# Gate and up products of batches 0 and 1 made joint, the short transform for batch 0, and new instruction sequences on every engine of a decoder layer

## What is computed

```
h = layernorm(x)
q, k, v = h Wq' + bq, h Wk' + bk, h Wv' + bv      # 16 heads of 16
qp, kp = elu(q) + 1, elu(k) + 1
attn = qp (kp' v) / (qp . sum(kp) + 1e-6)          # per head
x = x + attn Wo' + bo

score = (ctx Wq2' + bq2)(ctx Wk2' + bk2)' / 8 * layernorm(x)
x = x + softmax(where(mask, -inf, score))

h = fwht(layernorm(x) * SU_ug) / 64                # transform over 256
up, gate = h W_up' * s_up, h W_gate' * s_gate      # 256 -> 1024 each
h = fwht(silu(gate) * up * SU_dp) / 64             # transform over 1024
x = x + h W_down' * s_down                         # 1024 -> 256
```

## Time and profile before

| | |
|---|---|
| median of 3 runs | 125.3 us (125.2 to 125.59) |
| the profiled execution | 125.14 us |
| its span | 123.3 us |
| TensorE busy | 119.2 us, 97% |
| DVE, ACT, POOL busy | 82.7, 71.6, 68.5 us |

### The profile page before, as it was taken

The page is one execution under the profiler, slowest core; times in us unless marked ns, Lnnn a source line. Parts: engine busy times, 40 slices in busy tenths (PEclk is TensorE's granted clock), DMA queues, the critical chain, the costliest instruction groups (busy, mean ns, idle before and its releaser), DMA issues.

```text
span 123.3 us, 2272 instructions
## 1 busy us (share of the span) xinstructions
PE 119.2 (97%) x804; PEld 107.0 (87%) x804; DVE 82.7 (67%) x207; ACT 71.6 (58%) x158; POOL 68.5 (56%) x89
## 2 busy tenths in 40 slices
PE   5999999999999999999999999999999999999990
PEld 2259999999999999999989999988888888889890
DVE  1399989899889899899998959674522332220521
ACT  1785696679748689888491479983135444280000
POOL 2228959979979966959802605762005574066000
...
DMA packets 3823, 7.64 MB, mean 62 GB/s; under 512 B 544, under 2 KB 1952, under 8 KB 3684
## 3 DMA queue, kind: packets, MB, share of 16 engines
...
## 4 chain that ended last, share of the span: by engine, by line
PE 97%; POOL 0%; DVE 0%; issue 0%; POOLq 0%
PE bank L1283 19%; PE bank L1295 18%; PE bank L1300 11%; PE bank L1177 10%; PE bank L1304 5%; PE bank L1201 5%; PE bank L1239 5%; PE bank L1155 4%; PE bank L1115 4%; PE bank L1211 3%; PE bank L1221 3%; PE bank L1309 2%; PE bank L1146 2%; PE bank L1247 2%; PE bank L1128 1%; PE bank L1259 1%
## 5 line engine op out<-in xcount | busy, mean ns | idle before, releaser
L1283 PE MATMUL bank<-xh_home,wug 128*128 128x256 f32 x192 | 24.7, 285 | 0.0
L1283 PEld LDWEIGHTS bank<-xh_home,wug 128*128 128x128 f32 x192 | 23.6, 191 | 0.1
L1295 PE MATMUL bank<-xh_home,wug 128*128 128x512 f32 x96 | 22.0, 390 | 0.0
L1295 PEld LDWEIGHTS bank<-xh_home,wug 128*128 128x128 f32 x96 | 18.0, 188 | 3.7
L969 DVE SCALAR_TENSOR_TENSOR back<-bank,sc_up,back 128x512 f32<-128x512 f32 x8 | 6.0, 751 | 15.0 <-PE bank L1295 15.0
L351 POOL TENSOR_TENSOR hs<-back,hs 128x256 fp32r<-128x256 f32 x8 | 5.9, 740 | 17.0 <-ACT hs L614 16.9
L345 POOL TENSOR_TENSOR hs<-front,hs 128x256 fp32r<-128x256 f32 x16 | 11.5, 740 | 6.6 <-ACT hs L599 6.6
L1177 PE MATMUL bank<-watt,xT 128*128 128x256 f32 x96 | 14.0, 288 | 0.0
L1177 PEld LDWEIGHTS bank<-watt,xT 128*128 128x128 f32 x96 | 12.3, 189 | 0.9 <-ACT xT L492 0.7
L606 ACT ACTIVATE back<-bank,vecs 128x512 f32<-128x512 f32 x8 | 5.5, 688 | 12.1 <-PE bank L1295 12.1
L1300 PE MATMUL bank<-wdh,hs 128*128 128x512 f32 x48 | 12.5, 396 | 0.0
...
## 6 DMA issues: line engine op xcount, KB each, us to landing
...
```

The source lines that it names most:

```text
L1283: ins = mm(dst[:, n * SEQ:(n + 1) * SEQ], wug[:, wa, k, at_col + j * P:at_col + (j + 1) * P], xh[b][:, xb, k, :], start=(i == 0), stop=(i ...
L1295: ins = mm(dst[:, :].rearrange("p (b s) -> p b s", s=SEQ), wug[:, wa, k, at_col + j * P:at_col + (j + 1) * P], xh_home[:, PAIR, cols], sta ...
```

## The change

- Gate and up of batches 0 and 1 are joint as well: `gate_up(n)` for n = 0 to 15 replaces both old forms. Its first call waits for XH of both batches. `silu`, `hidden`, `h_hi` and `h_lo` work on the pair (the ring `sg` of 2 x 256 columns in `back`), and the odd batch of a pair has a tile `hs_odd` of its own.
- Batch 0's transform takes the short form; `mix` moves from the tile `ek` to `wo_raw`; `had_x` goes.
- `HEAD` and `SIDE` become one list `ORDER`; `down` is split in H (high products of a tile), L (low products), E (the last of the eight blocks) and F (the last tile). The sequences of DVE, ACT and POOL are new. J is `warm`: 8 before `mx`, then 1 and 5.

```
-HEAD = (("mx", 0), ("u", 0), ("T1", 0), ("u", 1), ("K", 0), ("V", 0), ("Q", 0), ("T1", 1), ("SC", 0),
...
+ORDER = (
+    ("J", 8), ("mx", 0), ("J", 1), ("J", 5), ("u", 0), ("T1", 0), ("u", 1), ("SC", 0), ("K", 0), ("V", 0), ("T1", 1),
+    ("Q", 0), ("ST", 0), ("K", 1), ("NUM", 0), ("V", 1), ("T1", 2), ("AT", 0), ("Q", 1), ("OUT", 0), ("ST", 1),
+    ("V", 2), ("NUM", 1), ("SC", 2), ("K", 2), ("AT", 1), ("Q", 2), ("T1", 3), ("OUT", 1), ("V", 3), ("SC", 1),
+    ("T3", 0), ("ST", 2), ("K", 3), ("NUM", 2), ("SC", 3), ("Q", 3), ("AT", 2), ("ST", 3), ("NUM", 3), ("T3", 1),
+    ("WD", 0), ("XH", 0), ("AT", 3), ("OUT", 2), ("WD", 1), ("XH", 1), ("WD", 2), ("OUT", 3), ("GG", 0), ("GG", 1),
+    ("GG", 2), ("GG", 3), ("GG", 4), ("WD", 3), ("GG", 5), ("GG", 6), ("GG", 7), ("T3", 2), ("H", 0), ("T3", 3),
+    ("L", 0), ("H", 1), ("XH", 2), ("H", 2), ("L", 1), ("E", 0), ("H", 3), ("XH", 3), ("L", 2), ("E", 1), ("E", 2),
+    ("L", 3), ("E", 3), ("GG", 8), ("GG", 9), ("GG", 10), ("GG", 11), ("GG", 12), ("GG", 13), ("GG", 14), ("GG", 15),
+    ("H", 4), ("H", 5), ("L", 4), ("H", 6), ("L", 5), ("E", 4), ("E", 5), ("L", 6), ("E", 6), ("F", 7),
+)
...
             def silu(n):
-                wait_full(act, "GU", n)
+                wait_full(act, "GG", n, 0)
                 if n == 0:
-                    act.wait_ge(s["ug_lo"], 2)
+                    act.wait_ge(s["ug_lo"], 4)
                 if n >= RING:
-                    act.wait_ge(s["h_lo"], n - RING + 1)
+                    act.wait_ge(s["h_lo"], 2 * (n - RING) + 2)
...
+            def gate_up(n):
+                q, j = n // JB, n % JB
                 if j == 0:
+                    for b in range(2 * q, 2 * q + 2):
+                        wait_read(pe, "XH", b)
+                if n == 0:
+                    pe.wait_ge(s["ug_lo"], 2)
+                if n == JB // 2:
+                    pe.wait_ge(s["ug_lo"], 4)
+                for t, at_col in enumerate((INTER, 0)):
+                    dst = take("GG", n, t)
                     for i, (k, wa, xb) in enumerate(PASSES):
                         cols = slice(xb * FB * SEQ + k * SEQ, xb * FB * SEQ + (k + 1) * SEQ)
                         ins = mm(dst[:, :].rearrange("p (b s) -> p b s", s=SEQ), wug[:, wa, k, at_col + j * P:at_col + (j + 1) * P],
+                                 xh_home[:, 2 * q:2 * q + 2, cols], start=(i == 0), stop=(i == len(PASSES) - 1))
+                    done(ins, "GG", n, t)
```

More of the change, by code:

```diff
@@ L32 @@
 BANKS = 8
-WARM, WARM_MORE = 8, 2
 MASKED = 3.0e35
@@ L650, in _ @@
+            exp_q(2)
             xT_hi(3)
-            at_hi(1)
-            negate_mean(3, 0)
-            score_evac(2)
-            exp_q(2)
             normalise(3, 0, xn3)
+            ug_hi(2)
+            table(ACT.Exp, 1)
+            mix_in(0)
+            ug_hi(3)
+            prob(1)
             x3_hi(0)
+            exp_k(3)
             score_evac(3)
-            exp_k(3)
-            prob(1)
+            exp_q(3)
+            at_hi(2)
+            pre_hi(0)
+            negate_mean(3, 1)
@@ L660, in _ @@
+            normalise(3, 1, xn3)
+            pre_hi(1)
+            mix_in(1)
+            x3_hi(1)
+            wd_hi(0)
             xh_hi(0)
-            ug_hi(2)
-            exp_q(3)
-            pre_hi(0)
+            at_hi(3)
+            xh_hi(1)
+            wd_hi(1)
             silu(0)
-            pre_hi(1)
-            negate_mean(3, 1)
+            wd_hi(2)
+            prob(2)
             silu(1)
-            ug_hi(3)
             silu(2)
-            normalise(3, 1, xn3)
-            table(ACT.Silu, 0)
@@ L688, in _ @@
             h_hi(5)
-            silu(6)
+            normalise(3, 2, xn3)
             h_hi(6)
+            mix_in(2)
+            normalise(3, 3, xn3)
             silu(7)
-            table(ACT.Exp, 1)
-            at_hi(3)
-            prob(2)
+            x3_hi(2)
+            mix_in(3)
+            x3_hi(3)
+            xh_hi(2)
             h_hi(7)
-            negate_mean(3, 2)
-            normalise(3, 2, xn3)
-            mix_in(2)
-            prob(3)
+            xh_hi(3)
             silu(8)
@@ L991, in _ @@
             ln_stats(1, 2)
-            u_lo(0)
+            ctx_lo(0)
+            elu_k(0)
+            ln_stats(1, 3)
+            v_add(0)
+            xT_lo(1)
             u_lo(1)
-            elu_k(0)
-            v_add(0)
-            ln_stats(1, 3)
-            xT_lo(1)
+            diagonal(0)
             elu_q(0)
-            dve.wait_ge(ld['cst'], 16)
-            diagonal(0)
-            ctx_lo(0)
+            ctx_lo(1)
+            attend(0)
             wo_lo()
-            attend(0)
             elu_k(1)
+            at_lo(0)
+            xT_lo(2)
             v_add(1)
-            xT_lo(2)
-            at_lo(0)
-            ctx_lo(1)
             elu_q(1)
@@ L1252, in hadamard_x @@
                 if b == 0:
-                    pe.wait_ge(s["had_ready"], 3)
+                    pe.wait_ge(s["had_ready"], 1)
                 dst = take("XH", b)
-                if b:
-                    pe.wait_ge(s[f"mix_lo{b}"], 1)
-                    for part in range(2):
-                        ins = mm(dst[:, :], had_d[:, :], x3T[:, b % 2, part, :, :].rearrange("p f s -> p (f s)"), start=(part == 0),
-                                 stop=(part == 1))
-                    done(ins, "XH", b)
-                    return
```

534 lines of the change are left out of this document (201 added, 333 removed), and 3 rows, old and new, of the table HEAD.

## The result

| | before | after |
|---|---|---|
| median | 125.3 us (125.2 to 125.59, 4 runs) | 133.61 us (133.18 to 134.09, 4 runs) |
| ratio to before | | 1.0664, 95% interval 1.0642 to 1.0685 |
| profiled execution, span | 125.14, 123.3 us | 133.37, 130.2 us |

The changed kernel is 6.6% slower, 8.3 us, where 1.3%, 1.6 us, was forecast. The direction was right, the size was not, and the time lies outside the range.

What follows compares the result with a forecast made beforehand. TensorE was taken as the bound before, with DVE holding the first joint product until 53.54 us; adding 21.81, 0.46 and 13.12 put the second half 1.57 us later, so 125.3 + 1.57 = 126.9 us, range 124.2 to 128.3.

Steps and rivals of the forecast that it cites:

- The bound: Kernel before the change: TensorE, busy 119.2 of 123.3 us, bounds it, so each saved product or new wait counts fully.
- What TensorE saves: Gate and up of batches 0 and 1 take 1.2 us less, the transform of batch 0 0.5 us less.
- What the start costs: Four more products on zeros, less 0.36 us of waiting at K, shift the head by +0.55 us.
- When DVE lets it go: First joint product waits for `xh_lo(1)` on DVE until 53.5 us; TensorE, ready at 50.97, waits about 2.6 us.
- DVE's queue as the limit: DVE's operations ahead of `xh_lo(1)`, 6.34 us beyond those done by 48.00 us, hold the first joint product.
- From there to the second joint half: After the first joint product, 21.81, 0.46 and 13.12 us put the second half at 88.93 us, 1.57 later than before.
- The term of T3 2: TensorE's possible wait at T3 2, before the second joint half: counted as nothing, up to 1.3 us above.
- The tie of 21.6 against 22.27 us: Ahead of T3 2, DVE's 21.6 us, waits included, against 22.27 of TensorE: a near tie, no wait counted.
- Table loads: ACT's four more, 1.28 us each: two hidden at the start, two delaying `hidden`, whose banks TensorE needs only later.
- A: TensorE stays the bound: first joint product at 50.97 us, 124.3 us in all; chance 17%.
- B: DVE idles nowhere and the new products on zeros shift nothing it does: 52.49 us, giving 125.8 us; chance 15%.
- C: First joint half waits too: `prob(2)`, `prob(3)` and loads make T3 2 or T3 3 1.3 us late, 128.2 us; 15%.

## Why the prediction was right or wrong

- **The bound.** Right: TensorE without waits before, so each new wait counts.
- **What TensorE saves.** Right. Five joint steps take 70.18 - 56.52 = 13.66 us, 0.228 per product. The Trainium skill's figure ("TensorE: Matmul & The Clock Gate", section "Back-to-back issue gap"), 2.5 ns beside N / 2.4, is too low here: 0.228 us leaves 0.014. (The list under the change counts ST 3 among the steps that moved ahead; it stood ahead of the first gate and up product before too, and the sum rightly leaves it out.)
- **What the start costs.** Wrong in the profiled execution. On the timeline the first u started at 6.25 us, 6.15 before, and NUM 0 at 17.55, 17.42 before: a shift of +0.13 us, not +0.55. In the traces of three other versions the first u came at 6.9 to 7.2 us, and there 0.9 is about right. What was missed is that this shift decides a collision.
- **When DVE lets it go.** This is the step that failed first. The list of operations was complete, and so was their order, and up to `at_lo(2)` at 44.92 us the trace follows it. But `pre_lo(0)` was priced by its row of before, 1.22 us, and took 3.41, because the new order put POOL's `ug_lo(1)` beside it. The sum took only DVE's rows and never asked what POOL did beside each of them. POOL's timeline of the kernel before had shown the effect, in a butterfly of 2.89 us that began 0.04 us behind DVE's `ctx_lo(1)` (22.24 us, 0.68), where others of its size take 2.4:

```profile
22.28 2.89 POOL L329 TENSOR_TENSOR wd_b<-wd_a 128x1024 f32<-128x1024 f32 x1
```

With this collision gone the product starts 9.22 us behind NUM 3, which is 54.3 us from the NUM 3 of `after`, against a forecast of 53.54: 2.2 of the 3.0 us were this one term. What is left goes with `x3_lo(1)` on POOL, which `pre_lo(1)` blocks: XH 1 waits 1.2 us for it. With these two parted as well the product waits 1.05 us for `xh_lo(1)` on DVE instead and comes no earlier (9.13 us behind NUM 3, with WD 2 moved away). The prediction named XH 1 as a place of waiting and priced only DVE.
- **DVE's queue as the limit.** Half right. It was long enough to be one, but 3.6 us less of it gave 0.15 us. Two paths end almost together there, and a sum over one engine doesn't see the other.
- **From there to the second joint half.** The term of T3 2 was mis-sized: counted as nothing, up to 1.3, it measured 1.62 in `after`, 2.30 once the first product was earlier, and 1.6 us in all where it was spread over later steps. The tie of 21.6 against 22.27 us compared DVE's work with TensorE's. The chain that matters passes ACT, DVE and POOL in turn, with two pairs of table loads in it, and does not shorten when one engine has time to spare. It begins with `silu(0)`, whose table load waits for `ug_lo(3)` on POOL, a wait that stands in the change and that the prediction did not look at; the blocked `pre_lo(0)` makes `ug_lo(3)` late as well, and so T3 2.
- **Table loads.** "Covered" was wrong. Two more of them cost 4.4 us.
- **The rivals.** A needed DVE 2.1 us faster than its rows and B needed it to idle nowhere; both fell. C was right in mechanism and place; it came on top of a later first product, and its 15% was too little for something called a near tie. No case held two delays at once, and none a collision, so the range ended at 128.3 us.

Not settled: why time less span varies by up to 1.4 us, why the rate on zeros rises 0.6 us earlier in some executions, and why the granted clock falls at T3 2 in one trace and not in another behind the same wait.
